# Edge chain of a graph kernel: first tile written out, gathers issued at once, rows turned by transposes

## The reference

```python
def L0(x, agg, pairs, Wq, bq, Wk, bk):           # attention over listed pairs
    q = (x[sub] @ Wq.T + bq).reshape(-1, 8, 64)
    k = (x[obj] @ Wk.T + bk).reshape(-1, 8, 64)
    att = ((q * k).sum(-1) / 8).T
    scores = zeros((8, n, n)).at[:, sub, obj].set(att)
    scores = where(agg == 0, -inf, scores)       # then the diagonal is set to 1e-7
    return softmax(scores, axis=2).sum(0) / 8 @ x

def L1(x, A):                                    # A = adj
    a = (A + A.T) * 0.5 + I
    deg = a.sum(1); a = deg**-0.5 [:, None] * a * deg**-0.5 [None, :]
    return (1e-8 * ones) @ a @ x                 # called with Coefficient2 = A

x = layernorm(x + L0(x, adj, ...)); x = layernorm(x + L1(x, adj, adj))
```

## Time and profile before

| | us |
|---|---|
| median of 3 runs (315.80 to 315.94) | 315.87 |
| the profiled execution, device time | 315.7 |
| the profiled execution, span from first to last instruction | 314.2 |
| PE busy | 205.5 |
| VectorE busy | 147.0 |
| ScalarE busy | 86.1 |
| GpSimd busy | 91.4 |
| mean granted TensorE clock | 0.821 |

### The profile page before, as it was taken

The page is one execution under the profiler, slowest core; times in us unless marked ns, Lnnn a source line. Parts: engine busy times, 40 slices in busy tenths (PEclk is TensorE's granted clock), DMA queues, the critical chain, the costliest instruction groups (busy, mean ns, idle before and its releaser), DMA issues.

```text
span 314.2 us, 3138 instructions
## 1 busy us (share of the span) xinstructions
PE 205.5 (65%) x883; PEld 86.9 (28%) x883; DVE 147.0 (47%) x379; ACT 86.1 (27%) x133; POOL 91.4 (29%) x107
## 2 busy tenths in 40 slices
PE   0077121222222269999999969999728399999992
PEld 0023000000000014444444454443313044444440
DVE  5987594100000000698385662007676644539642
ACT  4066662000000000876345300310200222205422
POOL 5777877777777300000000000204500100000000
PEclk9999655555555558999999978999957699999997
DMA  5999997000000000019945000201801190002312
GB/s 191 347 371 363 314 395 256 0 1 0 0 0 0 0 0 0 0 6 332 312 156 173 0 0 2 69 0 34 277 15 55 56 331 0 2 0 100 135 52 68
DMA packets 16075, 34.67 MB, mean 110 GB/s; under 512 B 3960, under 2 KB 4086, under 8 KB 16062
## 3 DMA queue, kind: packets, MB, share of 16 engines
q1 hardware_dynamic: 12526, 30.73, 28.6%
q0 software_dynamic: 3536, 3.79, 4.3%
HBM read 25.66 MB, written 8.86 MB: 110 GB/s over the span
## 4 chain that ended last, share of the span: by engine, by line
PE 59%; issue 28%; DVE 9%; ACT 1%; DVEq 1%; POOL 1%; ACTq 0%; POOLq 0%
PE ps L661 29%; PE ps L625 9%; PE ps L637 8%; PE ps L693 5%; PE ps L753 2%; DVE work L1016 2%; PE ps L781 2%; PE ps L710 1%; PE ps L763 1%; ACT xs L614 1%; DVE work L1122 0%; DVE m_new L1124 0%; DVE work L1103 0%; PE ps L750 0%; DVE rank L1010 0%
## 5 line engine op out<-in xcount | busy, mean ns | idle before, releaser
L661 PE MATMUL ps<-terms,at 128*128 (+1 forms) x242 | 68.5, 423 | 69.2 <-issue 68.8
L446 POOL DMA_INDIRECT kept<-in_adj_t,at_idx x79 | 77.4, 980 | 25.4 <-issue 23.8
L661 PEld LDWEIGHTS ps<-terms,at 128*128 (+1 forms) x242 | 24.4, 102 | 113.0 <-issue 91.2
L956 DVE SCALAR_TENSOR_TENSOR xs<-xs,ratio,u 128x512 f32<-128x512 f32 x11 | 7.6, 749 | 67.6 <-ACT u L529 67.5
L693 PE MATMUL ps<-terms,bm 128*128 128x512 f16 x132 | 33.3, 412 | 1.2 <-DVE slots L1068 1.2
L625 PE MATMUL ps<-terms,at 128*128 128x512 f16 x132 | 30.6, 385 | 0.4 <-DVE terms L1251 0.4
L529 ACT ACTIVATE u<-ps,scale 128x512 f32<-128x512 f32 x11 | 6.6, 694 | 82.2 <-PE ps L661 82.2
L457 POOL CAST so_i<-slots 128x2 int32 x2 | 0.4, 188 | 91.0 <-DVE slots L1068 90.9
L661 PE MATMUL ps<-terms,bm 128*128 (+1 forms) x110 | 23.9, 379 | 0.0
L637 PE MATMUL ps<-terms,at 128*128 128x512 f16 x110 | 23.9, 379 | 0.0
L693 PEld LDWEIGHTS ps<-terms,bm 128*128 128x128 f16 x132 | 13.6, 105 | 19.1 <-issue 7.3
(11 more groups left out here) (242 smaller groups left out, 240.5 us busy)
## 6 DMA issues: line engine op xcount, KB each, us to landing
work<-in_adj SPq DMA_DIRECT2D x6, 677.0 KB
bm<-in_adj_t SPq DMA_DIRECT2D x5, 677.0 KB
u<-in_adj_t SPq DMA_DIRECT2D x4, 677.0 KB
stage<-in_adj SPq DMA_DIRECT2D x4, 677.0 KB
u_rows<-u SPq DMA_DIRECT2D x10, 257.5 KB
x_rows<-xs SPq DMA_DIRECT2D x10, 256.0 KB
xs<-x_rows SPq DMA_DIRECT2D x10, 256.0 KB
out<-xs SPq DMA_DIRECT2D x10, 256.0 KB
```

Source lines behind the costliest of these rows:

```text
L446: pool.indirect_dma_start(out=kept[:, c:c + 1], out_offset=None, in_=adj_flat, in_offset=bass.IndirectOffsetOnAxis(ap=at_idx[:, c:c + 1], ...
L661: m = pe.matmul(ps[:, bank_of(i), :], matrix[:, bass.ds(k, 1), i * P:(i + 1) * P].rearrange("p o n -> p (o n)"), terms[:, s, bass.ds(k, 1) ...
L956: dve.scalar_tensor_tensor(xs[:, i, :], xs[:, i, :], ratio[:, i:i + 1], u[:, i, 0:H], ALU.mult, ALU.add).then_inc(v_step, 1)
```

## The change

The loops over tiles are split into a first tile that is written out with fixed addresses and a loop `later` whose body runs only for further tiles (none here), so each engine now skips these bodies. `scores` starts with columns 0 and 1e-7 beside the scores, so one DVE instruction makes all arguments of the exponentials. In particular:

- POOL waits for the first tile's indices (`first_i`, copied straight from PSUM) and issues six gathers at once: object and subject rows of x, the two adjacency rows, the row of `u_rows` and that of `x1_rows`. The iota `node_row` is issued once the x1 rows are stored. The gathered rows, and `node_row`, lie in the tile `xs`, which is free between the store and the reload of the first norm; the pair sums' result `bm_e` lies in `slot_cols`.
- Rows across partitions come from transposes of a broadcast column (`id_rows`, `score_rows`) and not from diagonals times ones; DVE adds the mask (`away`) to the transposed scores.
- The row sums are formed directly from gathered object rows: `share0`, a same-row matrix scaled by a coefficient, times `x_obj`, in one product; `v_rows`, its store and its load are gone. DVE forms the slot's own part (`own`) beside it.
- `moved` (the new first-norm row) is written after `dz` and not before.
- On PE, chunk 6 is cut in pieces of 4, 3 and 4 k-steps, chunk 7 in 4, 5 and 2, chunk 8 in 1 and 10; chunks 9 and 10 follow. ACT takes the chunks 7 and 8 out after the exponentials, and the root of the row's variance stands between 8 and 9.
- On DVE, four memsets stand ahead of the ranks, and the pair sums (`pair_sums`) and the scaling of `row_x0` stand before the products of the scores.

```diff
-            bx_chunk(6, 0, 6)
+            bx_chunk(6, 0, 4)
...
-            bx_chunk(6, 6, C)
+            bx_chunk(6, 4, 7)
             pack(EARLY)
             pack(last)
...
+            pool_wait(u_stored, STORED)
+            pool_wait(first_idx, 1)
+            gather(x_obj, x, first_i[:, 1:2], t_obj)
+            gather(x_own, x, first_i[:, 0:1], t_sub)
+            gather_rows(first_i)
...
+            def id_rows(sub1, key):
+                pe.transpose(ps[:, 5, 0:P], sub1.to_broadcast([P, P]), ident[:, :])
+                pe.transpose(ps[:, 5, P:2 * P], key.to_broadcast([P, P]), ident[:, :]).then_inc(id_row, 1)
...
+            def score_rows(column):
+                for h in range(HEADS):
+                    m = pe.matmul(ps[:, 6 + h // 4, (h % 4) * P:(h % 4 + 1) * P], column(h).to_broadcast([P, P]), ident[:, :],
+                                  is_transpose=True, start=True, stop=True)
+                m.then_inc(s_row, 1)
...
+            pe.wait_ge(l4_same, 1)
+            pe.matmul(ps[:, 6, :], share0[:, :], x_obj, start=True, stop=True).then_inc(l4_sum, 1)
...
+            bx_chunk(8, 1, C)
+            bx_chunk(9)
+            bx_chunk(10)
...
+        def later(eng, tiles, passed=None):
+            with eng.Fori(0, tiles) as t:
+                with eng.If(t > 0):
+                    yield t
+                    if passed is not None:
+                        eng.sem_inc(passed, 1)
...
+            def own_part(step, cf):
+                step(dve.scalar_tensor_tensor(own, x_own, cf[:, C_OWN:C_OWN + 1], x_own, ALU.mult, ALU.subtract))
+                step(dve.scalar_tensor_tensor(own, own_u[:, 0:H], cf[:, W_SELF:W_SELF + 1], own, ALU.mult, ALU.subtract))
```

More of the change, by code:

```diff
@@ L768, in _ @@
[L768 to L774 removed]
+            tiles = loop_tiles(pe)
+            with later(pe, tiles) as t:
+                for b in range(len(KEPT)):
+                    pack(b, t)
@@ L1044, in held @@
                 return table[:, bass.ds(t, 1), :].rearrange("p o f -> p (o f)")
[L1046 to L1061 removed]
+            dve.wait_ge(l1_packed, 1)
@@ L1077, in _, with products @@
+            main(dve.tensor_scalar(row_x0, row_x0, coefs[:, 0, CHANGE:CHANGE + 1], None, ALU.mult))
+            def products(step, t, into, done):
                 dve.wait_ge(l1_q, t + 1)
```

786 lines of the change are left out of this document (485 added, 301 removed).

## The result

The kernel after takes **300.38 us** in the median of four runs (298.99 to 301.53), the kernel before on the same chip 315.90 (four runs, 315.80 to 316.08). The ratio is 0.952, with a 95% interval of 0.949 to 0.955, so the change is worth 15.5 us. The profiled execution is the longest of the four: 301.53 us with a span of 299.6. What follows is on the clock of that span.

The account below looks back on a forecast made before the run. PE's chunks were taken as the bound once the chain shortens. First tail matmul at 234.9 plus 62.7 tail, 0.5 memsets and 0.3 clock gave a 298.4 us span, so 300.0 us; 8 in 10 range 297.5 to 305.

Parts of the forecast that it names:

- Start: Sign that the forecast is wrong: a stretch before 170 us changes length, which was assumed not to happen.
- Pack: Packing the first tile: it reaches DVE at 194.4, 1.4 us earlier (bounds 0.85 to 1.8).
- Memsets and iota: Four DVE memsets and POOL's iota ahead of the ranks: 0 to 1.3 us late, 0.5 taken.
- Gathers: POOL, after the tile: object gather begins at 195.4, object rows there at 198.8, subject rows 1.25 us later.
- Rival 2: DVE ahead of the scores' products: four more gathers hold the scores, 2 us late if the queue is slower, 302; 10%.
- Projections: PE's transposes, biases and projections after the gathers: 9.8 us, q ready at 208.6, 4.2 us earlier.
- rival 1: PE's granted clock falls inside the chain: 6.8 us at half clock costs up to 3.4 us, 303.4; 15%.
- Scores to exponentials: Products, eight transposes, mask, maximum, arguments, exponentials: 6.4 us in place of 11.75, done at 215.0.
- Exponentials to row sum: Small product, skip, DVE steps, `share0` and product with `x_obj`: row sum ends at 218.1, 17 us before to its start.
- rival 3: Skipped loops on each engine: 1.6 us each erases the gain, 2 gives 320; 3% slower than before, 4% some 306.
- From the row sum on: 64 PE matmuls of chunks 8 to 10 take 13.8 us to 231.9, `dz` 5.5 us early, tail at 234.9.
- Clock in the tail: PE's clock after its 2.1 us wait: between a gain of 0.6 and a loss of 1.7 us, loss of 0.3 taken.

Follow-up runs that it names:

- c_after2: The kernel after, unchanged, run once more as control beside a later group of kernels: median 300.17 us, chain 39.61 us.
- c_after: The kernel after, unchanged, run again as the yardstick of its group: median 300.74 us, chain 39.82 us.
- e_chunks_first: Kernel after with all of chunks 8, 9 and 10 put ahead of the row sum: 304.17 us.
- e_best: Kernel after with eight chunk 7 matmuls before the biases, pair sums and row scaling behind the slot's own part, chunk 10 behind two change products: 304.58 us.
- e_roundtrip: Kernel after with object rows stored to HBM and loaded back ahead of the row sum: 230.25 us on the chip where before takes 237.09.

## Why the prediction was right, and where not

300.0 was forecast and 300.38 measured. The mechanism is as it was told: PE's waits go from the chain, and chunks 8 to 10 cover the row. But in the profiled execution (299.6 us of span against 298.4) two larger terms went against each other, and in c_after2 (297.2) the steps met nearly by number. The marks, each on its own span; the ranks' first matmul (line 770) stands at 176.68 before, 175.57 in after and 176.81 in c_after2:

| step | forecast | after | c_after2 |
|---|---|---|---|
| tile on DVE | 194.4 | 194.06 | 194.63 |
| products of the scores | 208.6 | 210.95 | 208.54 |
| exponentials done | 215.0 | 217.05 | 214.6 |
| row sum done | 218.1 | 220.66 | 218.25 |
| chunks 8 to 10 done | 231.9 | 234.46 | 232.06 |
| first tail matmul | 234.9 | 237.50 | 235.09 |

**Start.** "A stretch before 170 us that has changed length" was named as what would upset the sum. In after the ranks came 1.1 us earlier than before. The stretch in which PE stands nearly still at half clock ended at 117.6 us there, and at 119.7 in before; in the three profiles of after's code it ends at 117.6, 120.0 and 120.9. So it varies between executions of one code, and this 1.1 us of the agreement is luck.

**Pack.** Off by 0.1 to 0.8 us. Forecast was a tile 1.4 us earlier. Measured from the ranks it is 0.6 earlier in after and 1.3 in c_after2. In after PE's six matmuls ran at half clock (2.38 us against 1.45), and DVE waited for the packs, not for its register. The prediction had said that these would be over by then; that holds only at the full clock.

**Memsets and iota.** 0.5 was forecast, 0 measured: the iota ran at 171.61 beside the second memset, which took 0.58 us as the first did without it, and DVE still waited 0.61 us for PE at 176.00. The price of 1.26 us for a copy beside an iota did not come up here.

**Gathers.** The object gather began 0.96 us behind the start of the copy of its indices, 1.0 forecast. Rival 2 (gathers hold the scores) is true by 0.4 us in an execution without a fall, where it had been put at nothing or at 2.

**Projections, rival 1.** 9.8 us forecast. In c_after2 they took 9.2 (198.88 to 208.10), in after 12.55 (198.31 to 210.86). This rival was given 15%, with 303.4 as its time. It came true in 1 of the 3 profiles of this code. In the projections it cost the 3.4 us of its price (12.55 for 9.2); 3.0 to 3.2 reached the chain, since without the fall the gathers hold it for 0.4. What was wrong is the way it was set apart: as a case that the kernel is in or not, whereas it varies from one execution to the next and moves each by 1%. The Trainium skill (TensorE: Matmul & The Clock Gate, Part 4: PE-mode transpose) says that a transpose doesn't count as PE-busy the same way. The same transposes in the same order stood in after, with the fall, and in c_after and c_after2, without it, so that rule alone doesn't decide it here. Nor does the busy share of the stretch before (5.98 of 6.75 us and a fall, 5.49 of 6.80 and none). What goes with it, with one exception in ten profiles, is whether the half-clock stretch ahead of the chain still took in the six matmuls of chunk 6; the cause is open.

**Scores to exponentials.** 6.4 us forecast, 6.2 measured in after, and 6.1 from the start of the products in c_after2. The eight transposes were put at 1.3 us and took 1.09. The skipped loop behind the maximum was put at 0.3 and cost 0.58.

**Exponentials to row sum.** 3.1 forecast, 3.6 measured. The mis-sized term is the skip ahead of `zz`, 0.94 us for 0.3. The prediction had called a skip cheap because chunk 7 started 0.26 us behind the slots. That row doesn't price one: the code has PE's skip ahead of its wait for the slots, and PE had already been idle for 1.15 us when they came. Both skips are now shown by taking the loops out: 1.5 us in the chain in all, not the 1.6 us each of rival 3. By the Trainium skill's page (Runtime: NRT & Kernel Launch, Instruction fetch mechanics) a taken branch out of the fetched blocks stalls for a fetch; the idle time that went with the loops is 0.58 and 0.94 us, so no stall of the size that would have decided the sign is there. Whether these two are fetches no row tells.

**From the row sum on.** 13.8 us forecast, 13.97 measured; `dz` 5.5 us early forecast, 6.0 measured; e_chunks_first and e_best price that slack from both sides. The step to the tail, 3.0, took 3.04.

**Clock in the tail.** A loss of 0.3 forecast, a gain of 0.6 measured: PE's waits of 1.6 us there didn't bring a fall, in any profile of this code. The tail took 62.1 us against 62.7.

From the forecast's 234.9 the first tail matmul in after is off by 2.6. That is -1.1 for the start, +0.8 for the pack, -0.15 for the gathers, +2.75 for the projections, -0.2 up to the exponentials and +0.5 from there to the row sum. 0.6 of tail, the 0.5 of memsets and the 0.3 of clock bring it back to +1.2 of span.

**The gain, by its parts.** Of 14.0 us (251.52 to 237.50) 2.1 are there when the chain begins, 1.1 of them the start's luck. 10.8 are PE's waits, 14.5 us before and 3.7 after. The last 1.1 is what remains between the work in the two stretches. The row's norm (5.57 us) is shown by e_chunks_first, which brings back 5.32. That the 5.47 us ahead of L790 went with VectorE's combining of rows is read from the traces and wasn't tried. Rows by transposes are worth 2.2 us for the scores alone. The prediction listed the store and load among the 17 us before the row sum; they were in that stretch but under chunk 10, and their 6.5 us (e_roundtrip) don't belong to the 14.0. The prices of single things put back aren't shares of the gain and don't add up to it.

## To carry over

A row of independent matmuls behind a chain is a purse with an amount, here 6.0 us: write it down, and charge every edit to it, because three edits that gain 0.4 to 0.6, 0.3 to 0.5 and 1.8 to 2.0 us of the chain alone made it 4.9 longer together, 3.6 of it a wait that none had alone and 1.7 the clock that fell behind it. Price a round trip through HBM by the wait on the engine that needs it, and add what the clock loses in that wait: beside a chunk a trip of the same size left PE no wait, and it cost 6.5 us and 1.7 of clock with no chunk ahead of the row sum. When a median differs by 1%, compare a length inside the trace between profiles with the same granted clock before believing in a cause: the medians of the skipped loops differed by 4.3 us, where 1.2 to 1.5 could be traced to them.

## What the hardware showed unexpectedly

**The same kernel took 315.65 us on one chip and 237.09 on another.** (That is the kernel before.) The difference lies ahead of all that is changed here: the chain begins at 194.72 in after and at 116.65 in e_roundtrip, 78 us earlier. From 60 to 85 us, first in c_after, then in e_roundtrip on the second chip:

```profile
60.00:85.00 25.00, 5.26 (x9) 1.03 (x10) 0.73 (x6) 0.00 (x0) 18.90 (x21) 0.50 0.02 0
```

```profile
60.00:85.00 25.00, 25.00 (x118) 11.33 (x117) 21.75 (x68) 15.27 (x24) 19.21 (x20) 1.00 0.82 252
```

PE issues one matmul every 2.8 us, with no releaser in the trace, for some 80 us, at half clock, while POOL's indirect DMAs go on at the same pace on both. Why wasn't tried. It's the largest thing in this kernel on the slow chips, five times what the change gave.

**The granted clock of the same code differs from one execution to the next**, in a place where PE is busy for 80 to 90% of the stretch, and a fall of 6.75 us there costs 2.9 to 3.2 us.

**A skipped loop costs VectorE 0.58 and 0.94 us** at two places on the path, by rows that lose this idle time when the loop is taken out.
